# Score stacks of two attention layers in a half-group layout, keys stored once, query parts in a turned order

## The reference

```python
q = (layernorm(x) @ Wq.T + bq)      # 16 heads of 8 features; layer 0 also rotates q and k by position (rope)
k = (ctx @ Wk.T + bk)
v = (ctx @ Wv.T + bv)
scores = einsum('bhsd,bhtd->bhst', q, k) / sqrt(8)
attn = softmax(scores, axis=-1)
x = x + tanh(g) * (einsum('bhst,bhtd->bhsd', attn, v) merged over heads @ Wo.T + bo)
```

## Time and profile before

| | us |
|---|---|
| median of 3 runs | 1830.58 (1823.94 to 1838.63) |
| the profiled execution | 1843.18 |
| its span in the profile | 1841.5 |
| PE busy (share of span) | 1447.3 (79%) |
| DVE busy | 927.8 (50%) |
| ACT, POOL busy | 487.7 (26%), 406.3 (22%) |
| attention of layer 0 | about 5 to 270 |
| attention of layer 1 | about 437 to 678 |

### The profile page before, as it was taken

How to read it: one execution, slowest core, us unless ns; L and a number is a source line. 1 busy time by engine, 2 the same in 40 slices (tenths; PEclk the granted TensorE clock), 3 DMA queues, 4 the chain that set the end, 5 groups by cost and what they waited for, 6 DMA issues and landing times. The chain is left out here.

```text
span 1841.5 us, 27105 instructions
## 1 busy us (share of the span) xinstructions
PE 1447.3 (79%) x8879; PEld 916.7 (50%) x8880; DVE 927.8 (50%) x2546; ACT 487.7 (26%) x1166; POOL 406.3 (22%) x681
## 2 busy tenths in 40 slices
PE   4789886884789776896776328847399999999998
PEld 2567663442667654565675216635344444444443
DVE  4466537884556433334554403337444655565435
ACT  1455541121557541222221003215101110110101
POOL 3676500002556301000011251145100000000000
PEclk8798877996789877997776559979699999999999
DMA  6666630002676615000001011111120221122010
GB/s 186 160 154 142 146 92 1 0 0 67 161 169 154 141 29 222 0 0 12 17 17 58 11 47 46 44 50 55 46 107 32 98 98 58 41 98 98 29 70 12
DMA packets 135131, 136.59 MB, mean 74 GB/s; under 512 B 12086, under 2 KB 123126, under 8 KB 129782
## 3 DMA queue, kind: packets, MB, share of 16 engines
q1 hardware_dynamic: 128438, 127.66, 24.7%
q0 software_dynamic: 3328, 6.82, 1.1%
q10 hardware_dynamic: 3264, 0.79, 0.2%
HBM read 99.39 MB, written 34.87 MB: 73 GB/s over the span
## 5 line engine op out<-in xcount | busy, mean ns | idle before, releaser
L2446 DVE TENSOR_TENSOR l3f_weighted_T<-l3f_w_e,l3f_xnT 128x512 f32<-128x512 f32 x128 | 88.3, 691 | 128.8 <-PE psum L2197 114.5
L2197 PE MATMUL psum<-l3f_weighted_T,w_l3f_q 128*128 128x512 f32 x256 | 133.7, 604 | 16.1 <-DVE l3f_weighted_T L2446 14.4
L2197 PE MATMUL psum<-l3f_weighted_T,w_l3f_k 128*128 128x512 f32 x256 | 131.5, 595 | 0.0
L2197 PE MATMUL psum<-l3f_weighted_T,w_l3f_v 128*128 128x512 f32 x256 | 130.7, 592 | 0.0
L710 DVE TENSOR_REDUCE l1x_minus_max<-psum 128x4 f32<-128x512 f32 x128 | 85.8, 687 | 86.8 <-PE psum L373 86.1
L2206 PE MATMUL psum<-l3f_weighted_T,w_l3f_o 128*128 128x512 f32 x256 | 124.3, 624 | 1.7 <-DVE l3f_weighted_T L2446 1.7
L710 DVE TENSOR_REDUCE l0x_minus_max<-psum 128x4 f32<-128x512 f32 x128 | 85.6, 686 | 69.1 <-PE psum L373 68.3
L2446 DVE TENSOR_TENSOR l3f_weighted_T<-l3f_w_e,l3f_oT 128x512 f32<-128x512 f32 x128 | 88.4, 692 | 57.3 <-PE psum L2206 29.9
L531 ACT ACTIVATE l0x_probsT<-psum 128x512 f32<-128x512 f32 x128 | 73.9, 595 | 60.4 <-PE psum L386 53.5
L531 ACT ACTIVATE l1x_probsT<-psum 128x512 f32<-128x512 f32 x128 | 74.1, 594 | 41.6 <-PE psum L386 33.2
L111 POOL TENSOR_TENSOR l3f_ln_rstd<-l3f_ln_mean_var,eps 128x4 f32<-128x4 f32 x8 | 1.9, 242 | 356.4 <-DVE l3f_ln_mean_var L104 356.4
(11 more groups left out here) (469 smaller groups left out, 3038.5 us busy)
## 6 DMA issues: line engine op xcount, KB each, us to landing
l3f_w_e<-l3f_weights_scratch SPq DMA_DIRECT2D x32, 1024.0 KB, 4.7
l0x_k_scratch<-l0x_k_parts SPq DMA_DIRECT2D x24, 384.0 KB, 3.7
l0x_k_stack<-l0x_k_scratch SPq DMA_DIRECT2D x16, 576.0 KB
l0x_q_stack<-l0x_q_scratch SPq DMA_DIRECT2D x48, 192.0 KB
l1x_k_scratch<-l1x_k_parts SPq DMA_DIRECT2D x24, 384.0 KB, 5.1
l1x_k_stack<-l1x_k_scratch SPq DMA_DIRECT2D x16, 576.0 KB
l1x_q_stack<-l1x_q_scratch SPq DMA_DIRECT2D x48, 192.0 KB
w_l2f_w<-in_l2f_w SPq DMA_DIRECT2D x2, 2048.0 KB, 12.6
```

The source lines that it names most:

```text
L2197: ins = pe.matmul(bank[:, :], w[name][:, e, :], xe[:, e % 2, :], start=(e == 0), stop=(e == NE3 - 1))
L2446: dve.tensor_tensor(xe[:, e % 2, :], wE[:, g % 2, e, :], src, ALU.mult).then_inc(s_xe, 1)
```

## The change

The scratch in DRAM is laid out by halves: (2 groups in turn, 2 halves, blocks, 128, 256 columns), so that for one row (block, d) the 16 heads by 256 columns of a half are one run of 8 KB. The stacks get the layout [75 rows, 2 groups in turn, 2 halves, 16 heads, 256 columns], so that a row's half is one run of 8 KB there too. The rows of a stack are now (s, a, d): k has part a, q has part (s + a) mod 3, which gives the same 9 pairs. So the k scratch holds 3 blocks, written once per half, and the k load reads these 24 rows three times through a source that repeats them. The q scratch holds 5 blocks (0, 1, 2, 0, 1), written by two DMAs per half, and the load for s reads blocks s to s + 2. Each half has a semaphore for its stores. PE and ACT address the stacks with the new layout. On POOL `split("q", 1)` moves ahead of `split_max(0)`. The core of the diff:

```diff
-        scratch = {"k": nc.dram_tensor(f"{name}_k_scratch", (2, NPART, NPART, P, T), BF16).ap(),
-                   "q": nc.dram_tensor(f"{name}_q_scratch", (2, NPART, P, T), BF16).ap()}
-        stack = {n: sb(f"{n}_stack", [TROWS, 2, HEADS, T], BF16) for n in "kq"}
+        blocks = {"k": NPART, "q": 2 * NPART - 1}
+        scratch = {n: nc.dram_tensor(f"{name}_{n}_scratch", (2, 2, blocks[n], P, HALF), BF16).ap() for n in "kq"}
+        stack = {n: sb(f"{n}_stack", [TROWS, 2, 2, HEADS, HALF], BF16) for n in "kq"}
...
-        stores = {"k": NPART, "q": 1}
+        stores = {"k": 1, "q": 2}
...
             def store(n, g):
 
                 sp.wait_ge(s_parts[n], g + 1)
-                if n == "k":
-                    for b in range(NPART):
-                        sp.dma_start(scratch["k"][g % 2, :, b].rearrange("a p t -> p a t"), parts["k"][:, :, :])\
-                          .then_inc(s_stored["k"], 16)
-                else:
-                    sp.dma_start(scratch["q"][g % 2].rearrange("b p t -> p b t"), parts["q"][:, :, :])\
-                      .then_inc(s_stored["q"], 16)
+                for hf in range(2):
+                    to = scratch[n][g % 2, hf].rearrange("a p t -> p a t")
+                    sp.dma_start(to[:, 0:NPART, :], parts[n][:, :, half(hf)]).then_inc(s_stored[n][hf], 16)
+                    if n == "q":
+                        sp.dma_start(to[:, NPART:2 * NPART - 1, :], parts["q"][:, 0:NPART - 1, half(hf)])\
+                          .then_inc(s_stored["q"][hf], 16)
 
             def load(n, g, hf):
 
-                parts_stored(sp, n, g)
+                parts_stored(sp, n, g, hf)
                 if g >= 2:
                     sp.wait_ge(s_T, 4 * (GS * (g - 2) + 2 * hf + 2))
+                rows_of = lambda ap: ap.rearrange("a (d h) t -> (a d) (h t)", h=HEADS)
+                block_rows = NPART * HD
                 if n == "k":
-                    sp.dma_start(stack["k"][0:SROWS, g % 2, :, half(hf)],
-                                 scratch["k"][g % 2].rearrange("a b (d h) t -> (a b d) h t", h=HEADS)[:, :, half(hf)])\
+                    sp.dma_start(stack["k"][0:SROWS, g % 2, hf, :, :].rearrange("r h t -> r (h t)"),
+                                 bcast(rows_of(scratch["k"][g % 2, hf]).unsqueeze(0),
+                                       [NPART, block_rows, HEADS * HALF]))\
                       .then_inc(s_stack["k"][g % 2][hf], 16)
                 else:
-                    rows_of_a = NPART * HD
-                    for a in range(NPART):
-                        sp.dma_start(stack["q"][a * rows_of_a:(a + 1) * rows_of_a, g % 2, :, half(hf)],
-                                     scratch["q"][g % 2].rearrange("b (d h) t -> (b d) h t", h=HEADS)[:, :, half(hf)])\
+                    for s in range(NPART):
+                        sp.dma_start(stack["q"][s * block_rows:(s + 1) * block_rows, g % 2, hf, :, :]
+                                     .rearrange("r h t -> r (h t)"), rows_of(scratch["q"][g % 2, hf, s:s + NPART]))\
                           .then_inc(s_stack["q"][g % 2][hf], 16)
...
@@ (POOL, split)
-                parts_stored(pool, n, g - 1)
+                for hf in range(2):
+                    parts_stored(pool, n, g - 1, hf)
...
             split("k", 1)
+            split("q", 1)
             split_max(0)
-            split("q", 1)
             split_max(1)
```

More of the change, by code:

```diff
@@ L230, in heads_attention @@
         s_split = sem("split_step")
-        s_stored = {n: sem(f"{n}_parts_in_dram") for n in "kq"}
+        s_stored = {n: [sem(f"{n}_parts_in_dram_{hf}") for hf in range(2)] for n in "kq"}
         s_stack = {n: [[sem(f"{n}_stack_in_{p}_{hf}") for hf in range(2)] for p in range(2)] for n in "kq"}
@@ L253, in heads_attention, with parts_stored @@
         half = lambda hf: slice(hf * HALF, (hf + 1) * HALF)
+        of_seq = lambda c: slice((c % 2) * P, (c % 2 + 1) * P)
         loads = {"k": 1, "q": NPART}
-        stores = {"k": NPART, "q": 1}
+        stores = {"k": 1, "q": 2}
         def stack_landed(eng, n, g, hf):
             eng.wait_ge(s_stack[n][g % 2][hf], 16 * loads[n] * (g // 2 + 1))
-        def parts_stored(eng, n, g):
-            eng.wait_ge(s_stored[n], 16 * stores[n] * (g + 1))
+        def parts_stored(eng, n, g, hf):
+            eng.wait_ge(s_stored[n][hf], 16 * stores[n] * (g + 1))
         block = ctx.enter_context(nc.Block())
@@ L269, in _ @@
             sp.wait_ge(s_fill, 4)
-            sp.dma_start(stack["k"][SROWS:TROWS, :, :, :].rearrange("a p h t -> a (p h) t"),
-                         bcast(ones_row[:, :].unsqueeze(1), [NPART, 2 * HEADS, T])).then_inc(s_ones, 16)
+            sp.dma_start(stack["k"][SROWS:TROWS, :, :, :, :].rearrange("a p f h t -> a (p f h) t"),
+                         bcast(ones_row[:, 0:HALF].unsqueeze(1), [NPART, 4 * HEADS, HALF])).then_inc(s_ones, 16)
             def store(n, g):
                 sp.wait_ge(s_parts[n], g + 1)
-                if n == "k":
-                    for b in range(NPART):
-                        sp.dma_start(scratch["k"][g % 2, :, b].rearrange("a p t -> p a t"), parts["k"][:, :, :])\
-                          .then_inc(s_stored["k"], 16)
-                else:
-                    sp.dma_start(scratch["q"][g % 2].rearrange("b p t -> p b t"), parts["q"][:, :, :])\
-                      .then_inc(s_stored["q"], 16)
+                for hf in range(2):
[4 more added lines that the diff above has]
+                          .then_inc(s_stored["q"][hf], 16)
@@ L372, in scores @@
                     h = 4 * u + i
-                    ins = pe.matmul(bankS[u % 2][:, seq(i)], stack["q"][0:SROWS, g % 2, h, seq(c)],
-                                    stack["k"][0:SROWS, g % 2, h, seq(c)], start=True, stop=True)
+                    ins = pe.matmul(bankS[u % 2][:, seq(i)], stack["q"][0:SROWS, g % 2, c // 2, h, of_seq(c)],
+                                    stack["k"][0:SROWS, g % 2, c // 2, h, of_seq(c)], start=True, stop=True)
                 ins.then_inc(s_S, 1)
@@ L385, in scoresT @@
                     h = 4 * u + i
-                    ins = pe.matmul(bankT[u % 2][:, seq(i)], stack["k"][:, g % 2, h, seq(c)],
-                                    stack["q"][:, g % 2, h, seq(c)], start=True, stop=True)
+                    ins = pe.matmul(bankT[u % 2][:, seq(i)], stack["k"][:, g % 2, c // 2, h, of_seq(c)],
+                                    stack["q"][:, g % 2, c // 2, h, of_seq(c)], start=True, stop=True)
                 ins.then_inc(s_T, 1)
@@ L524, in max_rows @@
                 act.wait_ge(s_mT, j + 1)
-                act.dma_start(stack["q"][SROWS:TROWS, g % 2, :, seq(c)], mT[:, seq(c)]).then_inc(s_mrow[c], 16)
+                act.dma_start(stack["q"][SROWS:TROWS, g % 2, c // 2, :, of_seq(c)], mT[:, seq(c)]).then_inc(s_mrow[c], 16)
             def exps(j, u):
```

## The result

The changed kernel takes 1893.7 us (median of 4 runs, 1892.9 to 1896.0), the kernel before on the same chip 1831.2: **a ratio of 1.034 [1.030, 1.039], 3.4% slower**. The profiled execution took 1893.52 us with a span of 1891.9, 50.4 us over the 1841.5 of before; the medians lie 62.5 us apart, since the profiled execution of before, 1843.18 us, was 12 us above its median. The forecast was 1845 us, the range ended at 1880.

The account below looks back on a forecast made before the run. Stack DMAs, a serial chain on SP's queue, were taken to set the time at both starts and in parts of layer 1; 6 + 2 + 1.7 + 2.4 + 2 = +14 us gave 1845 us, range 1800 to 1880.

Parts of the forecast that it names:

- Engines of the k load: Load of the k stack: its source begins with a repetition of 3, so it runs on 3 engines instead of 12.
- the chain in layer 1, redone: Layer 1's stack stores and loads on SP's queue: +1.0 us per period, +6 us over six periods (-6 to +18).
- rival 2: Three engines serving the k load become the bound, periods 26.3 to 28.2 us or more: +35, 1866 us, chance 0.27.
- the 8 KB row at 0.312 us everywhere: Stack loads: 403 GB/s at share 0.96 over 16 engines, 26.2 GB/s each, so 0.312 us per 8 KB row.
- Layer 0, +2: Layer 0's stack chain, same sum as layer 1 for group 4: +2 us over six periods (0 to +9).
- Cover is 1.5 us: Layer 0, group 4: PE could start at 146.2 but comes by itself at 147.7, so stacks have 1.5 us to spare.
- Starts: First groups: layer 0 first scores at 43.2, group 1 at 67.3, +1.7 us (0 to +4.4); layer 1 +2.4 (0 to +5).
- Rows of maxima, +2: ACT's DMA of maxima: 16 rows behind 8 KB rows cost 5.0 us, just inside the time: +2 us (-3 to +15).
- Rival 1, spread load, 1806: The k load runs on 12 engines or more after all, stack waits vanish: -25, 1806 us, chance 0.15.
- The 6 us given back for a lower clock: Spread-load case: -31 reduced to -25, since a layer 1 period without stack wait lasted as long, clock 0.87 against 0.99.
- rival 3: Rows of maxima arrive late, some 30 sequences a layer wait 0.3 to 0.5 us: +25, 1856 us, chance 0.10.
- The split ahead of the maxima, the indexing, the second wait: GpSimd's earlier q split, indexing by c // 2 and waiting for both halves' stores in split: each counted as nothing.

Follow-up runs that it names:

- e1: Changed kernel with the k load of a half issued as three DMAs of 24 rows, no repeated source, each on 12 engines: 1805.7 us, ratio 0.988.
- e10: Changed kernel with the k load's repetition moved to the middle dimension and q loads to every third partition, k load on 12 engines: 1790.6 us, ratio 0.980.
- e7: Changed kernel with keys stored three times again (9 blocks) and one plain k load of 72 different rows on 12 engines: 1814.5 us, ratio 0.990.
- e8: Kernel before the change with only keys stored once and a repeated source for the k load, rows of 512 B: 1962.4 us, ratio 1.068.
- e11: Changed kernel with q loads written to every third partition, k load still on three engines, scores wrong: 1895.7 us, ratio 1.038.
- e9: Changed kernel with the k load kept in 2 KB pieces by a pad in the k stack, still on three engines: 1893.5 us, ratio 1.036.
- e12: The kernel of e1 sent again in another batch: 1802.6 us, ratio 0.985.
- e4: Changed kernel with the old GpSimd order, split_max(0) ahead of split q of group 1: 1896.6 us, ratio 1.037.
- The probes: Changed kernel plus eight probes behind its end, each four loads differing in partitions, source or row size; 72 plain rows took 14.59 us, repeated source 32.70.

## Why the prediction was wrong, point by point

- **Engines of the k load: right.** 3, by two packet differences (e1, e10). It decides the case: e1, e7 and e10 undo it in three ways and land at 1806, 1814 and 1791 us, and e8 alone adds 130 us to the kernel before.
- **The failed step: the chain in layer 1, redone, +1.0 us a period (bounds -1 and +3); measured +3.8.** It was rival 2's mechanism, the three engines as the bound, which the prediction priced at +35 and gave 0.27. Its own sum of 24.6 to 26.5 us of work on these engines lay across the 25.4 us from which it decides, and its reserve, rows that slow down in full work (30 to 32 us), is what happened, at its lower end: the six periods of layer 1 are 28.5 to 30.1 us long, those of layer 0 28.3 to 34.3.
- **The term that was mis-sized: the 8 KB row at 0.312 us everywhere.** It came from a DMA over 128 partitions. While q rows move, 12 engines (share 0.77 of 16) carry 175 GB/s, 14.2 per engine at that share, 0.58 us a row; alone, the three engines carry 81 GB/s at 0.20, 25.3 each and 0.32 us a row (the rows at e11). In the 6 us shown each engine passes about 10 rows, of q and of k: 10 x (0.58 - 0.31) = 2.7 us of the 4.7 by which the period of 30.2 missed its sum of 25.5. The step from the first scores to load k, in which these rows lie ahead of it, missed by as much: 11.8 us instead of 9.1. The rest, 2.0 us in the two steps behind, was not taken apart.
- **Layer 0, +2: measured +15.6.** Same step. "Cover is 1.5 us" and "the queue ends just as the next store comes" left no room for dearer rows; the periods went to 28.3 us and more, the sign that the prediction named for full engines.
- **Starts.** The first scores of layer 0 came at 43.1, predicted 43.2; group 1 at 72.6, predicted 67.3: its load k was issued at 53.8, not after a store at 50.4, and load q 12.5 us later. Layer 1's +2.4 was +4.5, inside its bounds.
- **Rows of maxima, +2.** Their delay was foreseen (16 rows behind 8 KB rows) but the wait it made is 64.5 us, not a few. As a term of the sum it is small at most: e9 takes the wait away and leaves the time, with room for some 12 us.
- **Rival 1, spread load, 1806.** With the condition made true it gives 1806, 1803 (e1, e12) or 1791 (e10). The first scores of layer 0 start at 33.8 (e1) and 34.3 (e10), not 32. The 6 us given back for a lower clock did not come: in the six periods of layer 1 the clock rose from 0.89 to 0.96 and 0.99.
- **A reading that does not hold.** "PE's products are slower after a gap", in rival 3, rests on two rows that both stand behind a gap: the four products of 0.38 us follow 3.96 us of idling, those of 0.59 us 2.94.
- **The split ahead of the maxima, the indexing, the second wait: nothing**, as said (e4 for the first).

One feedback was in no term. Idle PE time came with a lower granted clock: 0.99 with 12.2 us idle (e10), 0.89 with 23.4 (before), 0.86 with 39.8 (after), and PE's busy time for the same products went 118.5, 131.4, 137.7. So a late stack came with a cost beyond its own length, 6.3 us in the six periods, and one in time with a gain. That the idling itself lowered the clock is not shown: of two single periods the one with 2.9 us of idling had 0.87, the one with 7.5 us had 0.99.

## What to carry to other kernels

Ask first on how many engines each side of a DMA lets it run, and only then how long its rows are: here rows 16 times longer on a quarter of the engines lost 3.4%, and the same rows with the repetition moved from the outermost to the middle dimension won 2%. When a chain runs through a few engines, add up their whole period, with the price of a row taken from a stretch with the same partitions and the same neighbours; if the sum comes within a few us of the period, forecast the bound. And where a wait appears at a small transfer that shares engines with a large one, shorten the large one before moving the small one: it shows the shortage, but curing it moves the wait.

## What the runs showed that was not expected

- **Rows on 12 engines are slower than on 3 or 16**: 0.49 to 0.58 us for 8 KB against 0.31. The Trainium skill (page SBUF — State Buffer, section "Door 1: The DMA port swizzle (why `[64,N]` ≈ `[32,N]`)") says that bandwidth depends on how many of the memory's 16 ports the partitions reach. By its formula and its 27.2 GB/s a port, the port that gets most rows of a load gets 4 for 24 adjacent partitions, 3 at a step of 3, 2 at a step of 5 and 8 for 72 partitions, which gives as an estimate 4.8, 3.6, 2.4 and 9.6 us for the four loads of a probe. The probes, less 2.9 us, took 4.3, 3.5, 2.8 and 11.7: the order is as the rule has it, and the sizes agree within some 20%. The kernel's rows don't test the rule, since its three q loads together write partitions 0 to 71 in either form (175 GB/s adjacent, 172 at a step of 3). They are near the 72-partition probe, 0.58 and 0.53 us a row against 0.49; what makes the rest stays open.
- **Two queues on one engine take turns, one row each.** In 138 to 143 us q10's 256 B rows and q1's 8 KB rows pass the same three engines at the same pace:

```profile
q1 hardware_dynamic: 52, 0.37, 17.5%
...
q10 hardware_dynamic: 50, 0.01, 1.1%
```

  So a small row waits for one large row, 0.3 us, and 16 of them for 5 us, the size that the prediction had worked out.
- **The issue of a DMA depends on its form**: three q loads 1.13 us with adjacent partitions, 2.25 us at a step of 3 (2.40 before).
